# Two-layer cross-attention and mixture-of-experts kernel: where LN2's inverse deviation lies, who scales the identities, the order of copies and low parts, and the size of GpSimd's subtractions

## The chip, the cores and the metric

One core of a Trainium2 chip. The metric is the device time of one execution in microseconds (us). TensorE (PE), VectorE (DVE), ScalarE (ACT), GpSimd (POOL) and the queues of SyncE (SP) each follow their own list of instructions and meet through semaphores.

## The reference, cut to what matters

```
x: 4 x 256 x 256, context: 4 x 256 x 128
q, k   = ctx @ Wq.T + bq, ctx @ Wk.T + bk
x      = x + tanh(g_x) * (LN(x) contracted with softmax(q k^T))      # attention, 4 batches
y      = LN(x)                                                       # "LN2"
logits = gelu(y @ rw1) @ rw2;  probs = softmax;  top-2 of 8 experts
x      = x + tanh(g_f) * sum over the two choices of p_e * (gelu(y @ w1[e] + b1[e]) @ w2[e] + b2[e])
         (tokens that did not choose an expert get its constant term instead)
```

1024 tokens, hidden size 1024, 8 experts, exact GELU.

## The kernel before, in words

Attention and layer norms run over four batches b of 256 tokens (two tiles t of 128). Per batch: `energies` (PE), `maxima` (DVE), `exps` (ACT), `shares` (DVE: reciprocal of the row sums, then two scaled identities `diag`, 128x128, in SBUF), `probT_tr` (PE, a product with the scaled identity, which transposes and divides at once), `probT_copy` (ACT), `mix` (PE), `residual` (DVE), `second_stats` (DVE), `second_deviation` (ACT, a square root), `second_norm` (DVE: reciprocal of the deviation, then two subtract-and-multiply instructions into `lnx`), `xnT_tr` and `router_hidden` (PE), `router_gelu` (ACT), `router_logits` (PE). `first_pull` (DVE) makes the scale `pull` of LN1 and, by one more instruction, `shift`, which only the constant term at the end reads.

The expert weights come in 32 quarters of 128x1024 fp32 through `stage`, a ring of 6 slots filled by the SP queue in order. Each quarter is split in two: the high part `w_hi` (f16, a copy: `high` on ACT, `own` on POOL) and the low part `w_lo` (bf16, stage minus w_hi: `low` on DVE, line 685, whole quarters; `lows` on POOL, line 399, in pieces of `PIECE` columns). Quarter q+6 is fetched only when both parts of quarter q are done. `DVE_QUARTERS` says which low parts DVE makes, `POOL_HIGHS` which high parts POOL makes. `wait_weights(engine, q)` waits until the low parts up to q are done on both engines.

The normalised tokens are split in the same way (`token_high` on ACT, `token_low` on POOL, line 412) and sent to a table in DRAM (`send`, line 575, one per batch). After the router, DVE finds the two experts of each token and every token's slot by a chain of small instructions (lines 821 to 861), PE turns them into row numbers, and POOL gathers the tokens of each block of 128 from the table (line 427), which needs `index_ready` and all four `table_sent`.

Then blocks of 128 rows pass through their expert. Blocks 0 to 7 (one for each expert, written out) use the weights in SBUF, later blocks (a loop) have their first weight matrix fetched by number. In iteration i, PE does `tokens_tr(i+1)` (line 1254) and interleaves `up(i, c)` (lines 1280 to 1282) with `down(i-1, c)` (lines 1291 to 1293) over eight column groups c. Each half of a hidden block goes through `gelu_half` and `hidden_high` on ACT and `hidden_low` on DVE (line 938), and `down` waits for them at c = 0 and c = 4. DVE's iteration i is: `xT_copy(i+2)`, `hidden_low(i, second half)`, low parts, a piece of the index work (`rest_of_blocks`, `rest_of_indices`, `experts_of_blocks`, `used_counts`, lines 884 to 961), `hidden_low(i+1, first half)`, `y_copy(i)`. POOL's later order of gathers, low parts and scatters (`put`) is written out by hand.

Of the kernel before, what the change touches and what calls it, by code (L numbers as in the profile page):

```python
# [4 lines left out]
P = 128  # L5
# [3 lines left out]
T = TOK // P  # L9
# [20 lines left out]
PIECE = 256  # L30
# [15 lines left out]
def flamingo_moe_kernel(nc, x, ctx_in, g_x, g_f, Wq, bq, Wk, bk, rw1, rw2, w1, b1, w2, b2, consts, out):  # L46
# [6 lines left out]
    with ctx:  # L53
# [64 lines left out]
        shift = sb("shift", [P, T], F32)  # L118
# [110 lines left out]
        q_done, k_done, q_ready, k_ready = sem("q_done"), sem("k_done"), sem("q_ready"), sem("k_ready")  # L229
        energy, max_ready, exp_ready, prob_ready = sem("energy"), sem("max_ready"), sem("exp_ready"), sem("prob_ready")  # L230
# [22 lines left out]
        DVE_QUARTERS = (6, 7, 8, 13, 14, 15, 17, 19, 20, 23, 24, 26, 28, 29, 30, 31)  # L253
        POOL_HIGHS = (0, 1, 2, 3, 4, 5, 9)
# [135 lines left out]
        def _(pool):  # L390
# [60 lines left out]
            own(0, 6)  # L451
            token_low(0)
# [4 lines left out]
            lows(10, 13)  # L457
# [46 lines left out]
        def _(act):  # L504
# [36 lines left out]

            def probT_copy(b):
# [62 lines left out]
            second_deviation(1)  # L605
            high(7, 8)
            xnT_copy(0)
            token_high(0)
            second_deviation(2)
            high(8, 9)  # L610
            xnT_copy(1)
            second_deviation(3)
            router_gelu(0)
            router_gelu(1)
            token_high(1)
            xnT_copy(3)
# [6 lines left out]
            send(1)  # L623
            send(2)
            high(11, 12)
            send(3)
            high(12, 13)
# [3 lines left out]
            high(13, 18)  # L631
# [18 lines left out]
            for i in range(NS):  # L650
                for half in range(2):
                    gelu_half(i, i % 2, i, half)
                    hidden_high(i, i % 2, half)
                    q = 18 + 2 * i + half
                    high(q, min(q + 1, QUARTERS))
# [19 lines left out]
        def _(dve):  # L675
# [39 lines left out]
            def shares(b):  # L715
                dve.wait_ge(exp_ready, 2 * b + 2)
                step(nc.vector.reciprocal(rinv[:, 2 * b:2 * b + 2], rsum[:, 2 * b:2 * b + 2]))
                for j in range(2):
                    last = nc.vector.tensor_scalar(diag[:, b, j, :], ident, rinv[:, 2 * b + j:2 * b + j + 1],  # L719
                                                   None, ALU.mult)  # L720
                last.then_inc(prob_ready, 1)
# [15 lines left out]
            def first_pull(h):  # L737
                ts = slice(4 * h, 4 * h + 4)
                dve.wait_ge(std_ready, h + 1)
                if h == 0:  # L740
                    dve.wait_ge(tg_ready, 1)
                step(nc.vector.reciprocal(rstd[:, ts], rstd[:, ts]))
                step(nc.vector.tensor_scalar(pull[:, ts], rstd[:, ts], tg[:, 0:1], None, ALU.mult))
                nc.vector.scalar_tensor_tensor(out=shift[:, ts], in0=mv[:, ts, 0], scalar=-1.0, in1=pull[:, ts],
                                               op0=ALU.mult, op1=ALU.mult)
# [17 lines left out]
            def second_norm(b):  # L763
                dve.wait_ge(std_ready, b + 3)
                if b == 0:
                    dve.wait_ge(zero_sent, 32)
                step(nc.vector.reciprocal(rstd2[:, 2 * b:2 * b + 2], rstd2[:, 2 * b:2 * b + 2]))
                for t in (2 * b, 2 * b + 1):
                    nc.vector.tensor_scalar(lnx[:, t, :], xs[:, t, :], mv2[:, t, 0:1], rstd2[:, t:t + 1],  # L769
                                            ALU.subtract, ALU.mult).then_inc(xn_ready, 1)  # L770
# [37 lines left out]
            low(8)  # L808
# [73 lines left out]
            def rest_of_blocks():  # L882
                rank_te = rank_s[:, :].rearrange("p (t e) -> p t e", t=T)
# [5 lines left out]
                step(nc.vector.tensor_reduce(out=st_[:, :], in_=ltc, axis=X, op=ALU.add))  # L889
                step(nc.vector.tensor_tensor(out=slotb, in0=rank_te, in1=e_bc(st_[:, :]), op=ALU.add))  # L890
# [104 lines left out]
            low(13)  # L995
            low(14)
# [85 lines left out]
        def _(pe):  # L1082
# [216 lines left out]
            for i in range(NS):  # L1299
# [34 lines left out]
            wait_weights(pe, QUARTERS - 1)  # L1334
# [4 lines left out]
            jl, used = last_pair(pe), used_blocks(pe)  # L1339
            with pe.Fori(JS, JN - 1) as j:  # L1340
# [84 lines left out]
```

## Time and profile before

| what | value |
|---|---|
| median of 3 runs | 204.19 us (201.62 to 208.66) |
| the profiled execution: its own time | 201.4 us |
| its span, first to last instruction | 199.5 us |
| granted TensorE clock, mean | 0.939 |
| PE busy | 162.1 us (81%) |
| DVE busy | 137.9 us (69%) |
| POOL busy | 111.6 us (56%) |
| ACT busy | 101.7 us (51%) |

Busy times are sums over stages of different nature: attention and router up to 44 us, choice of experts up to 60 us, written-out blocks up to 112 us, the loop of blocks up to 179 us, and the sum of outputs. 1.9 us of the execution lie around the span.

### The profile page before, as it was taken

To read this page: it belongs to the slowest core of one execution; us is meant where nothing else is said; L and a number is where in the kernel's file an instruction comes from. 1 tells how busy PE (TensorE), PEld (TensorE's weight loads), DVE (VectorE), ACT (ScalarE), POOL (GpSimd) and SP (SyncE) were. 2 spreads that over 40 slices of the span, in tenths; PEclk is the share of its full clock that TensorE was granted. 3 is DMA by queue.
4 is the path that set the end of the run, shared out by engine and by line. 5 is a ranking of instruction groups with operands and counts; after the bars stand their busy time and mean duration, and the time that the engine had idled before them with its cause. 6 is when DMAs were issued, how large, how long until landed. Compare 5 with 4: busy or idle time off the path is not lost.

```text
span 199.5 us, 5205 instructions
## 1 busy us (share of the span) xinstructions
PE 162.1 (81%) x1722; PEld 137.3 (69%) x1723; DVE 137.9 (69%) x304; ACT 101.7 (51%) x249; POOL 111.6 (56%) x172
## 2 busy tenths in 40 slices
PE   6887984593838999789899499699499999998910
PEld 2456873371318999679899499599399999886600
DVE  2679999998843567997987256945656777364184
ACT  0695746777822999938978244233244334430000
POOL 0049999979975989565975605544255444113200
PEclk9999999999585899969999999999999999999975
DMA  6899453349997288737119426655267656431395
GB/s 186 242 385 353 124 199 106 105 114 369 369 276 269 78 263 258 229 104 252 57 49 375 154 80 225 251 210 228 71 237 253 230 221 217 193 145 33 102 332 219
DMA packets 21028, 40.69 MB, mean 204 GB/s; under 512 B 2741, under 2 KB 12047, under 8 KB 21010
## 3 DMA queue, kind: packets, MB, share of 16 engines
q1 hardware_dynamic: 17680, 34.54, 49.0%
q0 software_dynamic: 1872, 4.73, 7.6%
q10 hardware_dynamic: 1458, 1.19, 1.8%
q8 instruction: 10, 0.16, 0.3%
q14 instruction: 8, 0.07, 0.1%
HBM read 23.66 MB, written 4.60 MB: 142 GB/s over the span
## 4 chain that ended last, share of the span: by engine, by line
PE 47%; DVE 29%; DMA 9%; issue 7%; ACT 3%; DVEq 1%; SPq 1%; POOL 1%; POOLq 0%
PE bank L1280 7%; PE bank L1282 7%; PE bank L1281 7%; PE bank L1291 7%; PE bank L1292 6%; PE bank L1293 6%; DVE w_lo L685 3%; DVE lnx L769 3%; DMA probT<-x_table,gidx 3%; DMA cf<-in_ctx 2%; DVE qT L719 2%; DMA stage<-y_table 2%; DVE lnT L938 2%; DVE xs L750 2%; ACT bank L639 2%
## 5 line engine op out<-in xcount | busy, mean ns | idle before, releaser
L639 ACT ACTIVATE bank<-bank,b1T 128x128 f32<-128x128 f32 x152 | 42.4, 342 | 56.8 <-PE bank L1282 56.6
L1291 PE MATMUL bank<-w_hi,cf 128*128 (+1 forms) x152 | 41.7, 275 | 7.9 <-DVE lnT L938 7.2
L399 POOL TENSOR_TENSOR w_lo<-stage,w_hi 128x256 bf16<-128x256 f32 x64 | 44.0, 720 | 0.9 <-ACT w_hi L515 0.2
L1292 PE MATMUL bank<-w_lo,cf 128*128 (+1 forms) x152 | 41.7, 275 | 0.0
L1293 PE MATMUL bank<-w_hi,lnT 128*128 (+1 forms) x152 | 41.7, 274 | 0.0
L1280 PE MATMUL bank<-cfT,stage 128*128 128x128 f16 x176 | 34.0, 219 | 0.0
L1282 PE MATMUL bank<-cfT,stage 128*128 128x128 f16 x176 | 34.0, 219 | 0.0
L1281 PE MATMUL bank<-cfT,stage 128*128 128x128 bf16 x176 | 34.0, 219 | 0.0
L938 DVE TENSOR_TENSOR lnT<-bank,cf 128x512 bf16<-128x512 f32 x38 | 26.2, 690 | 6.7 <-ACT cf L646 4.0
L416 POOL TENSOR_TENSOR held<-cst 128x1 f32<-128x1 f32 x31 | 6.0, 193 | 41.8 <-DVE lnx L951 40.7
L515 ACT ACTIVATE w_hi<-stage 128x1024 f16<-128x1024 f32 x25 | 26.2, 1049 | 3.2 <-DMA stage<-in_L_ffn_w 1.9
L1280 PE MATMUL bank<-cfT,w_hi 128*128 128x128 f16 x128 | 27.2, 233 | 0.6 <-DVE cfT L929 0.6
L1281 PE MATMUL bank<-cfT,w_hi 128*128 128x128 bf16 x128 | 27.3, 234 | 0.0
L1282 PE MATMUL bank<-cfT,w_lo 128*128 128x128 f16 x128 | 27.2, 234 | 0.0
L945 DVE CAST cf<-bank 128x512 f16<-128x512 f32 x22 | 15.1, 688 | 16.0 <-issue 9.8
L685 DVE TENSOR_TENSOR w_lo<-stage,w_hi 128x1024 bf16<-128x1024 f32 x16 | 21.4, 1369 | 0.0
L1291 PEld LDWEIGHTS bank<-w_hi,cf 128*128 128x128 f16 x152 | 15.0, 99 | 8.2 <-issue 7.4
L1280 PEld LDWEIGHTS bank<-cfT,stage 128*128 128x128 f16 x176 | 17.2, 98 | 0.9
L1281 PEld LDWEIGHTS bank<-cfT,stage 128*128 128x128 f16 x176 | 17.2, 98 | 0.9
L1282 PEld LDWEIGHTS bank<-cfT,stage 128*128 128x128 bf16 x176 | 17.2, 98 | 0.0
L929 DVE COPY cfT<-bank 128x256 int32<-128x256 int32 x20 | 8.4, 419 | 12.6 <-PE bank L1256 9.4
L1293 PEld LDWEIGHTS bank<-w_hi,lnT 128*128 128x128 bf16 x152 | 15.0, 98 | 1.8
(196 smaller groups left out, 341.9 us busy)
## 6 DMA issues: line engine op xcount, KB each, us to landing
stage<-in_L_ffn_w SPq DMA_DIRECT2D x32, 512.0 KB, 5.5
stage<-w_hi SPq DMA_DIRECT2D x12, 512.0 KB
stage<-w_lo SPq DMA_DIRECT2D x12, 512.0 KB
stage<-y_table SPq DMA_DIRECT2D x8, 256.0 KB, 4.3
xs<-in_x SPq DMA_DIRECT2D x2, 512.0 KB, 7.3
out<-stage SPq DMA_DIRECT2D x4, 256.0 KB, 2.8
cf<-in_ctx SPq DMA_DIRECT2D x1, 512.0 KB, 4.9
x_table<-cfT ACTq DMA_DIRECT2D x2, 256.0 KB, 5.6
```

The costliest lines, as they stand in the source:

```text
L399: last = nc.gpsimd.tensor_tensor(out=w_lo[:, q, n:n + PIECE], in0=stage[:, q % RING, n:n + PIECE], in1=w_hi[:, q, n:n + PIECE], op=ALU.sub ...
L515: nc.scalar.activation(w_hi[:, q, :], stage[:, q % RING, :], ACT.Copy).then_inc(hi_ready, 1)
L639: last = nc.scalar.activation(h, h, ACT.Gelu, bias=bias)
L685: nc.vector.tensor_tensor(out=w_lo[:, q, :], in0=stage[:, q % RING, :], in1=w_hi[:, q, :], op=ALU.subtract).then_inc(lo_dve, 1)
L938: nc.vector.tensor_tensor(out=h_lo[:, u, cs, :], in0=hidden_of(u, half), in1=h_hi[:, u, cs, :], op=ALU.subtract).then_inc(h_ready, 1)
L945: nc.vector.tensor_copy(h_hi[:, u, 4 * half:4 * half + 4, :], hidden_of(u, half)).then_inc(hh_ready, 1)
L1280: mm(o, wh, xh[:, d, :], start=(d == 0), stop=False)
L1281: mm(o, wh, xl[:, d, :], start=False, stop=False)
L1282: last = mm(o, wl, xh[:, d, :], start=False, stop=(d == DC - 1))
L1291: mm(o, h_hi[:, u, c, :], w2_hi[:, ex, 1, c, :], start=(c == 0), stop=False)
L1292: mm(o, h_hi[:, u, c, :], w2_lo[:, ex, 1, c, :], start=False, stop=False)
L1293: last = mm(o, h_lo[:, u, c, :], w2_hi[:, ex, 1, c, :], start=False, stop=(c == HC - 1))
```

## The change

`PIECE` goes from 256 to 512. LN2's reciprocal is written to PSUM (the start of the bank that the batch's `mix` used), and the normalisation becomes a scalar_tensor_tensor whose second tensor is that PSUM column, broadcast. The scaled identities move to ACT, after a new semaphore `rinv_ready` from DVE's reciprocal. `shift` is no longer made in `first_pull`; the instruction that writes the last column of `cat` makes it at the end. On ACT the copies of attention and LN2 (`xnT_copy`) go ahead of `high` and `token_high`, and one `high` more stands between `send`s. The low parts are dealt anew and, on DVE, one of them stands ahead of each `hidden_low` of the second half; the index work of iteration 2 is divided over iterations 1 and 2, and `used_counts` moves from iteration 5 to 4. PE waits for the weights of `down` in two steps, runs `rest_of_codes` at c = 1, not 3, and loads its registers for the loop before it waits for the last weights.

```
-PIECE = 256
+PIECE = 512
-DVE_QUARTERS = (6, 7, 8, 13, 14, 15, 17, 19, 20, 23, 24, 26, 28, 29, 30, 31)
-POOL_HIGHS = (0, 1, 2, 3, 4, 5, 9)
+DVE_QUARTERS = (6, 7, 11, 12, 13, 15, 17, 19, 20, 22, 23, 26, 28, 29, 30, 31)
+POOL_HIGHS = (0, 1, 2, 3, 4, 5, 9, 27)

 POOL:
 own(0, 6)
+lows(8, 9)
 token_low(0)
 own(9, 10)
 token_low(1); token_low(2); token_low(3)
-lows(10, 13)
+lows(10, 11)
...
+lows(14, 15)
+refill(6, 0, 2, 16)
 lows(16, 17)
-refill(6, 0, 2, 16)
-lows(18, 19)
 wait(yidx_ready, 1); put(0, 0); refill(7, 1, 3, 16)
+lows(18, 19)
+put(1, 1)
 lows(21, 22)
-put(1, 1)
-lows(22, 23)
 put(2, 0)
-lows(25, 26)
-put(3, 1)
-lows(27, 28)
+lows(24, 25)
 wait(index_ready, 2)
 refill(NS, 0, 4, 32)
+put(3, 1)
+lows(25, 26)
+own(27, 28)
 put(4, 0)

 ACT:
+def shares(b):
+    act.wait_ge(rinv_ready, b + 1)
+    for j in range(2):
+        last = nc.scalar.activation(diag[:, b, j, :], ident, ACT.Copy, scale=rinv[:, 2 * b + j:2 * b + j + 1])
+    last.then_inc(prob_ready, 1)
 exps(0); project(1)
+shares(0)
 exps(1)
+shares(1)
 probT_copy(0); exps(2)
+shares(2)
 exps(3); probT_copy(1)
+shares(3)
 ...
-high(7, 8)
 xnT_copy(0)
-token_high(0)
+high(7, 8)
 second_deviation(2)
-high(8, 9)
 xnT_copy(1)
+high(8, 9)
 second_deviation(3)
 router_gelu(0); router_gelu(1)
-token_high(1)
+token_high(0)
 xnT_copy(3)
+token_high(1)
 ...
 send(1)
+high(11, 12)
 send(2)
-high(11, 12)
+high(12, 13)
 send(3)
-high(12, 13)

 DVE:
 def shares(b):
     dve.wait_ge(exp_ready, 2 * b + 2)
-    step(nc.vector.reciprocal(rinv..., rsum...))
-    for j in range(2):
-        last = nc.vector.tensor_scalar(diag[:, b, j, :], ident, rinv[:, 2 * b + j:2 * b + j + 1], None, ALU.mult)
-    last.then_inc(prob_ready, 1)
+    nc.vector.reciprocal(rinv..., rsum...).then_inc(rinv_ready, 1)
 def second_norm(b):
-    step(nc.vector.reciprocal(rstd2[:, 2 * b:2 * b + 2], rstd2[:, 2 * b:2 * b + 2]))
+    inverse = bank[3 + b][:, 0:2]
+    step(nc.vector.reciprocal(inverse, rstd2[:, 2 * b:2 * b + 2]))
     for t in (2 * b, 2 * b + 1):
-        nc.vector.tensor_scalar(lnx[:, t, :], xs[:, t, :], mv2[:, t, 0:1], rstd2[:, t:t + 1], subtract, mult)
+        nc.vector.scalar_tensor_tensor(out=lnx[:, t, :], in0=xs[:, t, :], scalar=mv2[:, t, 0:1],
+            in1=inverse[:, t % 2:t % 2 + 1].broadcast_to([P, D]), op0=subtract, op1=mult)
-low(8)                                  # ahead of the choice of experts: low(6), low(7) stay
-low(13); low(14)                        # after the row numbers
+low(11); low(12)
 ...
-low(15)
+low(13)
-between = {0: (17,), 1: (19, 20), 2: (), 3: (23, 24), 4: (26,), 5: (28, 29), 6: (30, 31)}
+ahead = {0: (15,), 1: (19,), 2: (20,), 3: (22,), 4: (23,), 5: (26,), 6: (30,)}
+behind = {0: (17,), 5: (28, 29), 6: (31,)}
 for i in range(NS - 1):
     xT_copy(i + 2, u)
+    for q in ahead[i]: low(q)
     hidden_low(i, u, 1)
-    for q in between[i]: low(q)
+    for q in behind.get(i, ()): low(q)
+    i == 1: rest_of_starts()     # the first four instructions of what was rest_of_blocks
     i == 2: rest_of_blocks()     i == 3: rest_of_indices()
-    i == 4: experts_of_blocks()  i == 5: used_counts()
+    i == 4: experts_of_blocks(), used_counts()

 PE:
-if c == 0: wait_weights(pe, QPE * i - 1)
+if c % 4 == 0: wait_weights(pe, QPE * i - 2 + c // 4)
-if i == 4 and c == 3: ... rest_of_codes()
+if i == 4 and c == 1: ... rest_of_codes()
-wait_weights(pe, QUARTERS - 1)
 pe.wait_ge(eb_ready, 1)
 (two register loads, wait for used_ready, two more)
+wait_weights(pe, QUARTERS - 1)
```

## Rows read from the trace of the kernel before

**Rows 1.** Windows over blocks 0, 2, 4 and 7: busy by engine, granted clock, DMA.

```profile
60.69:65.90 5.21, 5.21 (x50) 5.21 (x51) 2.08 (x3) 2.42 (x6) 3.58 (x4) 0.50 0.55 200
...
71.67:77.19 5.52, 5.52 (x79) 5.25 (x76) 4.41 (x6) 5.16 (x13) 4.54 (x7) 1.00 0.79 241
...
82.71:92.31 9.60, 7.55 (x95) 6.83 (x93) 8.86 (x20) 5.32 (x13) 4.86 (x6) 0.82 0.51 160
...
104.25:112.33 8.08, 5.53 (x78) 5.00 (x74) 4.74 (x7) 6.08 (x16) 4.89 (x7) 1.00 0.82 309
```

**Rows 2.** The chain that ended last, around the gather: start, us, what.

```profile
53.34 0.17 DVE gidx L861
...
53.79 5.64 DMA probT<-x_table,gidx
```

**Rows 3.** DVE's timeline, 20 to 45 us: start, us, line, operation.

```profile
21.12 0.58 DVE L743 TENSOR_SCALAR pull<-rstd,tg 128x4 f32<-128x4 f32 x1
21.73 0.59 DVE L744 SCALAR_TENSOR_TENSOR shift<-mv,pull 128x4 f32<-128x4 f32 x1
...
23.58 0.86 DVE L750 SCALAR_TENSOR_TENSOR xs<-bank,pull,xs 128x256 f32<-128x256 f32 x2
...
26.70 1.69 DVE L769 TENSOR_SCALAR lnx<-xs,mv,rstd 128x256 f32<-128x256 f32 x2
...
37.74 1.24 DVE L769 TENSOR_SCALAR lnx<-xs,mv,rstd 128x256 f32<-128x256 f32 x2
...
39.50 5.44 DVE L685 TENSOR_TENSOR w_lo<-stage,w_hi 128x1024 bf16<-128x1024 f32 x3
```

**Rows 4.** DVE's instructions grouped by line and form: busy us, mean ns.

```profile
L769 DVE TENSOR_SCALAR lnx<-xs,mv,rstd 128x256 f32<-128x256 f32 x8 | 6.4, 835 | 0.1
L719 DVE TENSOR_SCALAR qT<-cst,rinv 128x128 f32<-128x128 f32 x8 | 5.3, 699 | 0.1
...
L750 DVE SCALAR_TENSOR_TENSOR xs<-bank,pull,xs 128x256 f32<-128x256 f32 x8 | 3.4, 469 | 0.0
```

**Rows 5.** ACT's timeline: the third load of a function table, and the last send.

```profile
20.93 1.28 ACT L580 ACT_TABLE_LOAD   x1
...
45.98 0.33 ACTq L575 DMA_DIRECT2D x_table<-probT  x1
```

**Rows 6.** The page's group of ACT's 128x128 activations.

```profile
L639 ACT ACTIVATE bank<-bank,b1T 128x128 f32<-128x128 f32 x152 | 42.4, 342 | 56.8 <-PE bank L1282 56.6
```

**Rows 7.** The DMA view, sends of the table: count, KB each, us to landing.

```profile
x_table<-probT ACTq DMA_DIRECT2D x2, 256.0 KB, 5.4
```

**Rows 8.** POOL's timeline, 32 to 46 us.

```profile
32.07 2.56 POOL L399 TENSOR_TENSOR w_lo<-stage,w_hi 128x256 bf16<-128x256 f32 x4
34.59 1.16 POOL L412 TENSOR_TENSOR cfT<-lnx,cfT 128x512 bf16<-128x512 f32 x1
...
42.02 3.93 POOL L412 TENSOR_TENSOR probT<-lnx,probT 128x512 bf16<-128x512 f32 x2 [1.40 <-ACT probT L571]
```

**Rows 9.** PE's timeline: the router's last product, and two waits (in brackets) between blocks.

```profile
43.01 0.61 PE L1176 MATMUL bank<-rw_s,qT 128*128 128x8 f32 x4
...
85.48 0.27 PE L1291 MATMUL bank<-w_hi,cf 128*128 128x256 f16 x1 [2.04 <-DVE lnT L938]
...
112.33 0.28 PE L1254 MATMUL bank<-ident,probT 128*128 128x128 f16 x2 [2.55 <-issue]
```

**Rows 10.** DVE's timeline in the written-out blocks.

```profile
73.32 0.69 DVE L938 TENSOR_TENSOR lnT<-bank,cf 128x512 bf16<-128x512 f32 x1 [0.69 <-ACT cf L646]
...
80.39 1.69 DVE L887 TENSOR_TENSOR lnx<-cst,more 128x72 f32<-128x72 f32 x1
...
84.65 0.68 DVE L938 TENSOR_TENSOR lnT<-bank,cf 128x512 bf16<-128x512 f32 x1
...
107.84 1.22 DVE L685 TENSOR_TENSOR w_lo<-stage,w_hi 128x1024 bf16<-128x1024 f32 x1
```

**Rows 11.** SP's timeline: the first fetch of a looped block's weights.

```profile
103.63 0.52 SPq L356 DMA_DIRECT2D stage<-w_hi  x1
```

More of the change, by code:

```diff
@@ L540, in exps @@
                                          accum_out=rsum[:, 2 * b + j:2 * b + j + 1]).then_inc(exp_ready, 1)
+            def shares(b):
+                act.wait_ge(rinv_ready, b + 1)
+                for j in range(2):
+                    last = nc.scalar.activation(diag[:, b, j, :], ident, ACT.Copy,
+                                                scale=rinv[:, 2 * b + j:2 * b + j + 1])
+                last.then_inc(prob_ready, 1)
             def probT_copy(b):
@@ L605, in _ @@
             second_deviation(1)
+            xnT_copy(0)
             high(7, 8)
-            xnT_copy(0)
-            token_high(0)
             second_deviation(2)
+            xnT_copy(1)
             high(8, 9)
-            xnT_copy(1)
             second_deviation(3)
@@ L630, in _ @@
             nc.scalar.activation(warm[:, 2:3], tg[:, 0:1], ACT.Gelu)
-            high(13, 18)
+            high(13, 17)
             def gelu_half(i, u, e, half):
@@ L653, in _ @@
                     hidden_high(i, i % 2, half)
-                    q = 18 + 2 * i + half
+                    q = 17 + 2 * i + half
+                    if q >= 27:
+                        q += 1
                     high(q, min(q + 1, QUARTERS))
@@ L716, in shares @@
                 dve.wait_ge(exp_ready, 2 * b + 2)
-                step(nc.vector.reciprocal(rinv[:, 2 * b:2 * b + 2], rsum[:, 2 * b:2 * b + 2]))
-                for j in range(2):
-                    last = nc.vector.tensor_scalar(diag[:, b, j, :], ident, rinv[:, 2 * b + j:2 * b + j + 1],
-                                                   None, ALU.mult)
-                last.then_inc(prob_ready, 1)
+                nc.vector.reciprocal(rinv[:, 2 * b:2 * b + 2], rsum[:, 2 * b:2 * b + 2]).then_inc(rinv_ready, 1)
             def lnT_copy(b):
@@ L743, in first_pull @@
                 step(nc.vector.tensor_scalar(pull[:, ts], rstd[:, ts], tg[:, 0:1], None, ALU.mult))
-                nc.vector.scalar_tensor_tensor(out=shift[:, ts], in0=mv[:, ts, 0], scalar=-1.0, in1=pull[:, ts],
-                                               op0=ALU.mult, op1=ALU.mult)
             def residual(b):
@@ L990, in constant_sum @@
                 nc.vector.tensor_tensor(out=cat[:, :, 0:N_EXP], in0=dcat[:, 0, :, :], in1=dcat[:, 1, :, :], op=ALU.add)
-                nc.vector.tensor_copy(cat[:, :, 2 * N_EXP:CAT], shift[:, :].unsqueeze(2))
+                nc.vector.scalar_tensor_tensor(out=cat[:, :, 2 * N_EXP:CAT], in0=mv[:, :, 0:1], scalar=-1.0,
+                                               in1=pull[:, :].unsqueeze(2), op0=ALU.mult, op1=ALU.mult)
                 nc.vector.tensor_tensor(out=cat[:, :, N_EXP:2 * N_EXP], in0=wprod[:, 0, :, :], in1=wprod[:, 1, :, :],
                                         op=ALU.add).then_inc(cat_ready, 1)
-            low(13)
-            low(14)
+            low(11)
+            low(12)
             scatter_rows(0, N_EXP)
@@ L1008, in _ @@
                 xT_copy(i + 2, u)
+                for q in ahead[i]:
+                    low(q)
                 hidden_low(i, u, 1)
-                for q in between[i]:
+                for q in behind.get(i, ()):
                     low(q)
-                if i == 2:
+                if i == 1:
+                    rest_of_starts()
+                elif i == 2:
                     rest_of_blocks()
@@ L1306, in _ @@
                     if i:
-                        if c == 0:
-                            wait_weights(pe, QPE * i - 1)
+                        if c % 4 == 0:
+                            wait_weights(pe, QPE * i - 2 + c // 4)
                         down(i - 1, 1 - u, i - 1, c)
-                        if i == 4 and c == 3:
+                        if i == 4 and c == 1:
                             pe.wait_ge(y_ready, 3)
```

14 lines of the change are left out of this document (7 added, 7 removed).

## The prediction

> **What bounds the kernel now.** I read the table of busy times first: PE is busy for 81%, so the blocks should be PE's and everything else a chain. The windows over single blocks bear this out [rows 1]: block 2 takes 5.52 us with PE busy throughout at full clock, block 4 takes 9.60 and block 7 takes 8.08, with PE idle for 2.0 and 2.5 us of them. PE's own timeline names the two waits [rows 9]: 2.04 us for DVE's low part of a hidden half, 2.55 us of "issue", which is PE's sequencer on register loads. Block 0 runs at half clock [rows 1]. Ahead of the blocks I followed the chain of waits: DVE from the residuals to the choice of experts, then the row numbers at 53.34 + 0.17 = 53.51, the gather from 53.79 [rows 2], and the first product of block 0 at 60.69. DVE is the bound there, and part of its time is no work: normalising 128x256 takes 0.84 us on average, while a two-tensor instruction of the same size, one of its tensors in PSUM, takes 0.47; a 128x128 scaling takes 0.70; even 4 columns of `pull` and of `shift` take 0.58 and 0.59 [rows 3, 4]. So instructions wholly in SBUF wait here for something, and POOL is subtracting all the while in pieces of 0.64 (2.56 for four) [rows 8]. In the blocks it is the same: 72 columns took 1.69 us [rows 10].
>
> **Attention and LN2.** DVE loses the eight scalings (5.3 us of busy time by the group; back to back a little less), two `shift`s (0.55 each on the path) and about 0.4 us of each of eight normalisations, 3.1 us in all if they cost what the residual's instruction costs [rows 4]. Not all of it shortens the path. ACT takes eight scalings. No row has ACT at 128x128 from SBUF; its nearest, 128x128 in PSUM, is 0.34 [rows 6], pipelined 0.28 to 0.3, so I take 0.3 to 0.35 each, 2.6 us in all, and the ends 0.25 and 0.5. Three of the four pairs also make a round trip (ACT's exps, DVE's reciprocal, ACT again), some 0.4 us in which ACT waits, and behind it are queued the next exps, the copies of `probT` and the square root with its table load, which was at 20.93 [rows 5]. Placing these by hand, the load comes at 22.5 to 22.8, 1.7 us later. On DVE the first residual was at 23.58 [rows 3]; now it follows the last reciprocal, at about 21.6. From there to the last normalisation's end at 37.74 + 1.24 = 38.98 [rows 3] it was 15.4 us; take off 0.55 for a `shift`, 3.1 for the normalisations, and add 2.2 for three places where DVE now runs out of work and waits for ACT's square roots. It ends at 21.6 + 13.95 = 35.6, 3.4 us earlier.
>
> From that end to the router's last product it took 4.64 us (43.01 + 0.61 [rows 9]), all of it PE and ACT, which now have their copies first: 40.2. DVE has its two low parts done by then, at the 1.81 us each of the three that stood there (5.44 / 3 [rows 3]): from 36.2 to 39.8. The choice of experts began at 39.50 + 5.44 = 44.94 and needs 53.51 - 44.94 = 8.57 us, all the same after: the row numbers are there at about 48.9, 4.6 us earlier.
>
> **The table takes over.** The gather needs the four sends too, and they hang on POOL. The last `token_low` ended at 42.02 + 3.93 = 45.95, the last send went at 45.98 [rows 5, 8] and landed 5.4 us later [rows 7], at 51.4, two us before it was needed. POOL's new list up to that `token_low` has one quarter more (`lows(8, 9)`), which waits for ACT's high part at about 33.7. Two pieces of 512 should cost what the `token_low` of 512 columns costs, 1.16 each [rows 8]: 2.3 for 2.56, so 0.26 off each of seven quarters, 1.8 in all, and 2.3 more for quarter 8. DVE's low parts fall into the same stretch: the `token_low`s that met them took 1.97, not 1.16 [rows 8]. I get the last `token_low` at 44.5 (no collision) to 46.5 (both low parts in the way) and take 45.5; ACT's sends stand behind three `high`s of about 1.05, ready at 44.9, and so don't decide. Sent at 45.8, landed at 51.2 to 51.5, gather at 51.8 for 53.79: **2.0 us gained** (1.0 to 3.3), not 4.6. PE then idles longer ahead of block 0; it is at half clock there anyway.
>
> **The blocks.** In iteration 2, DVE's index work kept the low part of block 3's first half until 84.65 [rows 10]. Four of its instructions, some 2.8 us, move to iteration 1, whose second low part goes; the low part then comes near 82.3, ahead of PE's need at 83.4. Block 4 gives back the wait of 2.04 and the half clock that followed it: 9.60 less 5.52 and less 0.6 for `rest_of_codes`, so **3.5 us** (2 to 3.6) [rows 1, 9].
>
> Against it: the low part moved ahead of each `hidden_low`. DVE sat idle there for 0.69 us until ACT was done [rows 10]; the low part takes 1.22 alone [rows 10] and 1.81 beside POOL. `hidden_low` comes 0.4 to 1.1 us late, and behind it wait the low part of the next half, `y_copy` and PE's `down` at c = 4. By the same timelines PE's slack there is 0.5 to 0.8. So nothing is lost where POOL is silent and up to 0.5 where it subtracts; iteration 1 with its four small instructions is the tightest, and low(29), behind three low parts, has 0.6 us left before block 7. I put **0.8 us** on this, from 0 to 3.
>
> Block 7's 2.55 us: the last low part ended at 107.84 + 1.22 = 109.06 [rows 10] and only then did PE's sequencer begin its loads, which lasted to 112.33 [rows 9], 3.3 us. With the wait behind them they start as soon as the queue has taken block 7's last products. How far ahead the sequencer is no row shows: at least the 0.7 us of work it had left at 109.06. The ends are a gain of 0 and of 2.55; two such loads in the loop of blocks cause no gap on PE, so I take 1.0. A full gain would soon meet the fetch for block 8, issued at 103.63 [rows 11], now one low part later.
>
> Later steps cost about nothing: POOL's 16 quarters are 4 us shorter under other waits, `shift` in `cat` has 8 columns, and the loop of blocks and the end are unchanged, PE-bound at 5.5 us a block.
>
> **Sum.** 201.4 - 2.0 - 3.5 + 0.8 - 1.0 = 195.7 for an execution like the profiled one. That one lies at the low end of the three runs, 2.8 us below their median. Some of this excess will be in the other median too; I take half: **197.0 us**, against 204.19.
>
> **A rule that speaks against the change.** The rows above show waiting instructions and a POOL that works in pieces. The Trainium skill, "SBUF — State Buffer", section "Who interferes with whom", says that the loser of the pair of ports that VectorE and GpSimd share waits for the winner's whole instruction. The trace agrees with waits of up to one or two pieces (1.69 us for 72 columns). By this rule a piece of 512 makes each remaining wait up to 0.5 us longer.
>
> **The rivals.**
> (A) Longer pieces hurt the blocks. DVE's low parts ahead of `hidden_low`, and the index work, wait for pieces of 1.16 instead of 0.64. For: DVE took 1.81 a quarter beside POOL's 512-column instructions. Against: in the blocks most low parts took 1.22, and POOL has pauses. If each of five iterations stalls PE by 1.2 us over its slack and the clock falls after each as in block 4 (1.5 us each, from 9.60 - 6.1 - 2.04), it costs 13.5 us: 201.4 - 2.0 - 3.5 - 1.0 + 13.5 = 208.4, slower; it decides from about 2 us a stall, when the clock goes too. Chance 0.07. Without loss of the clock (5 x 0.9 = 4.5 us) it is 199.4, with the excess 200.8, no change: 0.18.
> (B) The normalisation in its new form waits as before, the change doesn't do what it says. LN2 keeps its 3.1 us, the row numbers come at 52.0, the gather at 52.3 and not 51.8: 196.2, with the excess 197.5. The table hides nearly all of this. Chance 0.1.
> (C) The table isn't the bound, as POOL's shorter quarters bring it forward: gather at 49.2, 193.1, or 194.4 with the excess. Chance 0.15.
> (D) The gain at the front is spent: ACT becomes the bound in attention (scalings at 0.5, round trips at 0.6), the gather stays at 53.5, and iteration 1 stalls: 201.4 - 0.3 - 2.0 + 0.8 = 199.9, about 201 with the excess. Chance 0.1.
> My forecast: 0.4.
>
> **Range and chances.** Forecast, B and C lie between 192 and 200; A without the clock and D at 200 to 202. The range 192 to 202.5 leaves out A with the clock and the best ends. Two per cent, about what a measurement can tell from no change here, is 4.1 us, so 200.1 is the border. Faster: 0.4 + 0.1 + 0.15, and a little of A and D: 0.68; same 0.25; slower 0.07.
>
> **What would show it.** Normalisations of 0.45 to 0.5 us each; ACT's scalings at 0.3 to 0.35; a first residual near 21.6; row numbers near 49 and a gather that starts 2 to 3 us after them, released by the last send; no wait of 2 us on PE in block 4 and full clock in it; the gap before block 8 under 2 us. I would be wrong if DVE's low parts in the blocks take 1.8 us or more and PE waits for `hidden_low` in blocks 2 to 7, if POOL's 512-column pieces cost more than 1.3 us, or if the sends land before the row numbers.

## The result and the profile after

The changed kernel is slower by 1.3%: 204.86 us, median of 20 runs, against 202.88 for the kernel before on the same chip (20 runs); ratio 1.013, 95% interval 1.009 to 1.017. Here and below the medians take all executions and the ratios only those that did not fall into a slower state, so a ratio is not the quotient of the medians beside it. Forecast was 197.0 with a range of 192 to 202.5. The profiled executions stand at 204.87 (span 202.8) and 201.4 (span 199.5), so the traces have 3.3 us of span to explain.

**The front gained more than was forecast, in part by another way.** DVE's timeline, the group of the normalisations and ACT's group of the scaled identities (busy us, mean ns), and the sends of the table (KB each, us to landing):

```profile
21.99 0.86 DVE L759 SCALAR_TENSOR_TENSOR xs<-bank,pull,xs 128x256 f32<-128x256 f32 x2
...
34.50 0.87 DVE L779 SCALAR_TENSOR_TENSOR lnx<-xs,mv,bank 128x256 f32<-128x256 f32 x2
...
42.89 0.22 DVE L831 TENSOR_REDUCE top<-bank 128x8 f32<-128x64 f32 x1 [3.39 <-PE bank L1193]
...
51.38 0.16 DVE L871 SCALAR_TENSOR_TENSOR gidx<-code,bank 128x8 int32<-128x8 f32 x1
...
L779 DVE SCALAR_TENSOR_TENSOR lnx<-xs,mv,bank 128x256 f32<-128x256 f32 x8 | 3.5, 478 | 0.1
...
L547 ACT ACTIVATE qT<-cst,rinv 128x128 f32<-128x128 f32 x8 | 2.8, 394 | 0.9 <-DVE rinv L732 0.9
...
x_table<-probT ACTq DMA_DIRECT2D x2, 256.0 KB, 3.6
```

The normalisations cost 478 ns where they cost 835 [rows 4]; the last ends at 35.37, where it was 38.98 [rows 3]. The row numbers, though, come at 51.54, only 2.0 us earlier. DVE waited 3.39 us for the router. The reason is in PE's timeline and the windows:

```profile
32.57 1.13 PE L1186 MATMUL bank<-kT,rw_s 128*128 128x256 f32 x4 [1.45 <-ACT kT L567]
34.43 2.10 PE L1174 MATMUL bank<-cst,lnx 128*128 128x128 f32 x8 [0.73 <-DVE lnx L779]
...
37.04 2.05 PE L1186 MATMUL bank<-kT,rw_s 128*128 128x256 f32 x4
...
35.00:41.00 6.00, 6.00 (x22) 5.12 (x21) 4.29 (x4) 3.22 (x8) 5.43 (x4) 0.50 0.34 103
```

After the gaps of 1.45 and 0.73, TensorE's granted clock is 0.50 (1.2 of 2.4 GHz) from 35 to 41, and four router products take 2.05 us instead of 1.13. The last send goes at 46.11, where it went at 45.98 [rows 5], and by the view's 3.6 us (5.4 before [rows 7]) it lands at about 49.7, before the row numbers; the gather starts at 51.83 and block 0's tokens reach PE at 54.79, 4.7 us before the 59.47 of the kernel before. From the gather's start to its first rows it took 3.0 us, not 5.7.

**The blocks lost it again.** Windows, one row for each of blocks 0 to 7 (columns as in [rows 1]):

```profile
55.87:60.83 4.96, 3.06 (x53) 2.91 (x53) 2.00 (x3) 2.66 (x6) 3.37 (x4) 1.00 0.90 294
60.83:67.33 6.50, 5.68 (x79) 5.27 (x77) 6.08 (x4) 5.33 (x13) 6.30 (x6) 1.00 0.56 176
67.33:74.22 6.89, 5.69 (x79) 5.26 (x77) 5.68 (x11) 5.28 (x13) 3.82 (x5) 1.00 0.75 235
74.22:79.74 5.52, 5.52 (x78) 5.25 (x76) 5.32 (x5) 5.27 (x13) 5.34 (x6) 1.00 0.57 158
79.74:88.24 8.50, 6.08 (x94) 5.66 (x92) 8.16 (x18) 5.27 (x13) 4.29 (x5) 1.00 0.71 241
88.24:94.15 5.91, 5.69 (x78) 5.26 (x76) 5.84 (x9) 5.28 (x13) 5.22 (x7) 1.00 0.40 124
94.15:105.55 11.40, 7.36 (x78) 6.56 (x76) 9.83 (x19) 5.31 (x13) 8.26 (x9) 0.85 0.35 112
105.55:113.22 7.67, 5.70 (x79) 5.17 (x76) 4.74 (x7) 5.96 (x16) 4.28 (x7) 1.00 0.86 319
```

The same blocks took 5.53, 5.52, 5.52, 9.60, 5.52, 6.26 and 8.24 (blocks 1 to 7) before. Block 4 gives back 1.1 us, block 6 costs 5.1, blocks 1 and 2 cost 1.0 and 1.4. The lead of 5.3 us at block 1 is a lag of 0.9 at block 8. PE's timeline names what it waited for, and its group view sums it up:

```profile
82.88 0.27 PE L1308 MATMUL bank<-w_hi,cf 128*128 128x256 f16 x1 [2.42 <-DVE lnT L950]
...
98.95 0.27 PE L1308 MATMUL bank<-w_hi,cf 128*128 128x256 f16 x1 [4.04 <-DVE lnT L950]
...
113.22 0.28 PE L1271 MATMUL bank<-ident,probT 128*128 128x128 f16 x2 [1.98 <-issue]
...
PE bank L1308 <- DVE lnT L950: 13.4, 7, 4.0
```

Seven waits for `hidden_low`, 13.4 us in all; before there were four, 7.2 us. In blocks 1 and 2 PE waited 0.82 us (at 65.02) and 1.20 (at 69.25), behind two low parts of DVE that now stand near POOL's gathers and subtractions; alone a low part takes 1.22 [rows 10]:

```profile
61.60 2.68 DVE L700 TENSOR_TENSOR w_lo<-stage,w_hi 128x1024 bf16<-128x1024 f32 x1
...
64.80 3.71 DVE L700 TENSOR_TENSOR w_lo<-stage,w_hi 128x1024 bf16<-128x1024 f32 x1
...
65.12 2.29 POOL L399 TENSOR_TENSOR w_lo<-stage,w_hi 128x512 bf16<-128x512 f32 x2
```

What held DVE in the later blocks is seen when its timeline is laid beside POOL's, which is the main reading of this case:

```profile
77.00 3.09 DVE L902 TENSOR_TENSOR lnx<-rank_s,st_ 128x64 f32<-128x64 f32 x1
80.13 0.23 DVE L903 SCALAR_TENSOR_TENSOR lnx<-rank_s,lnx 128x64 f32<-128x64 f32 x1
...
85.45 2.31 DVE L882 TENSOR_SCALAR yt<-code 128x16 f32<-128x16 f32 x1
87.68 0.16 DVE L883 TENSOR_SCALAR yt<-code 128x16 f32<-128x16 f32 x1
...
91.55 3.81 DVE L921 TENSOR_TENSOR en<-en,cst 128x8 f32<-128x8 f32 x1
```

```profile
76.69 1.01 POOL L446 DMA_INDIRECT y_table<-lnx,yidx  x1 [0.16 <-issue]
77.72 2.29 POOL L399 TENSOR_TENSOR w_lo<-stage,w_hi 128x512 bf16<-128x512 f32 x2
...
85.41 2.31 POOL L399 TENSOR_TENSOR w_lo<-stage,w_hi 128x512 bf16<-128x512 f32 x2
...
91.04 1.00 POOL L446 DMA_INDIRECT y_table<-lnx,yidx  x1 [0.16 <-issue]
92.06 2.28 POOL L399 TENSOR_TENSOR w_lo<-stage,w_hi 128x512 bf16<-128x512 f32 x2
94.28 1.05 POOL L406 CAST w_hi<-stage 128x1024 f16<-128x1024 f32 x1
```

Eight columns of `en` take 3.81 us, and end at 95.36; POOL's unbroken run (issue of the scatter, two pieces, the cast) ends at 95.33. The other two: 80.09 against 80.01, 87.76 against 87.72. Once DVE is through, its next instruction of the same kind takes 0.16 to 0.23. So in these three cases DVE did not get in at the border between two pieces; it waited until POOL's run was over.

### The profile page after: what moved, and what is told of

Its sections match the earlier page's. It is cut to its first block, busy times and chain, and to the rows that moved or that the text cites. A ratio compares the mean times of both kernels' runs of the same rounds, so it can differ in the third digit from the quotient of the medians.

```text
span 202.8 us, 5180 instructions
## 1 busy us (share of the span) xinstructions
PE 165.6 (82%) x1722; PEld 139.8 (69%) x1723; DVE 137.4 (68%) x294; ACT 102.3 (50%) x256; POOL 107.7 (53%) x141
## 3 DMA queue, kind: packets, MB, share of 16 engines
q10 hardware_dynamic: 1458, 1.19, 1.7%
## 4 chain that ended last, share of the span: by engine, by line
PE 49%; DVE 28%; issue 7%; DMA 7%; ACT 4%; POOL 1%; DVEq 1%; SPq 1%; POOLq 0%
PE bank L1308 6%; PE bank L1298 6%; PE bank L1299 6%; PE bank L1297 6%; PE bank L1310 6%; PE bank L1309 6%; DVE w_lo L700 4%; PE bank L1105 3%; DMA probT<-x_table,gidx 3%; DVE lnT L950 3%; DMA stage<-y_table 3%; DVE en L921 2%; PE bank L1186 2%; DVE lnx L902 1%; DVE lnx L779 1%
## 5 line engine op out<-in xcount | busy, mean ns | idle before, releaser
L1308 PE MATMUL bank<-w_hi,cf 128*128 (+1 forms) x152 | 42.3, 278 | 13.4 <-DVE lnT L950 13.4
L399 POOL TENSOR_TENSOR w_lo<-stage,w_hi 128x512 bf16<-128x512 f32 x32 | 36.6, 1169 | 2.2 <-ACT w_hi L517 1.5
L1297 PE MATMUL bank<-cfT,stage 128*128 128x128 f16 x176 | 34.7, 222 | 0.0
L1298 PE MATMUL bank<-cfT,stage 128*128 128x128 bf16 x176 | 34.7, 222 | 0.0
L1299 PE MATMUL bank<-cfT,stage 128*128 128x128 f16 x176 | 34.6, 222 | 0.0
L416 POOL TENSOR_TENSOR held<-cst 128x1 f32<-128x1 f32 x31 | 8.3, 269 | 47.4 <-DVE lnx L963 46.4
L1297 PE MATMUL bank<-cfT,w_hi 128*128 128x128 f16 x128 | 25.1, 223 | 0.6 <-DVE cfT L941 0.6
L517 ACT ACTIVATE w_hi<-stage 128x1024 f16<-128x1024 f32 x24 | 24.9, 1047 | 0.9 <-POOL cfT L412 0.9
L1299 PE MATMUL bank<-cfT,w_lo 128*128 128x128 f16 x128 | 25.2, 224 | 0.0
L1298 PE MATMUL bank<-cfT,w_hi 128*128 128x128 bf16 x128 | 25.2, 224 | 0.0
L700 DVE TENSOR_TENSOR w_lo<-stage,w_hi 128x1024 bf16<-128x1024 f32 x16 | 24.3, 1534 | 0.0
L1309 PEld LDWEIGHTS bank<-w_lo,cf 128*128 128x128 f16 x152 | 15.1, 99 | 1.5 <-issue 1.4
```

The lines of the kernel that those rows point to most:

```text
L399: last = nc.gpsimd.tensor_tensor(out=w_lo[:, q, n:n + PIECE], in0=stage[:, q % RING, n:n + PIECE], in1=w_hi[:, q, n:n + PIECE], op=ALU.sub ...
L517: nc.scalar.activation(w_hi[:, q, :], stage[:, q % RING, :], ACT.Copy).then_inc(hi_ready, 1)
L700: nc.vector.tensor_tensor(out=w_lo[:, q, :], in0=stage[:, q % RING, :], in1=w_hi[:, q, :], op=ALU.subtract).then_inc(lo_dve, 1)
L1297: mm(o, wh, xh[:, d, :], start=(d == 0), stop=False)
L1298: mm(o, wh, xl[:, d, :], start=False, stop=False)
L1299: last = mm(o, wl, xh[:, d, :], start=False, stop=(d == DC - 1))
```

## The experiments

**My theory**: a DVE instruction wholly in SBUF waits to the end of POOL's unbroken run, and the index work pays for that; its cure is operands in PSUM. (Experiments 1 and 3 refute "to the end" as a rule, experiment 5 bears out the rest.) **Rivals**: the length of a piece alone is the price (a wait to the next border); the low part ahead of each `hidden_low` makes it late; the half clock in the router. Each kernel was compared with the kernel before on the same chip; the chips differ between groups of experiments, so two experiments are compared here by the difference of their ratios.

**1. The changed kernel with pieces of 256**

```
-PIECE = 512
+PIECE = 256
```

> The changed kernel with GpSimd's pieces back at 256 columns. Theory P (a VectorE instruction wholly in SBUF waits for GpSimd's running stream, and two long pieces leave it one chance to get in where four leave three): the waits of the changed kernel's blocks (2.68 and 3.71 us for two low parts, 3.09 for the 64 columns of line 902, 3.81 for 8 columns of line 921) fall to 2 us or less each, PE's 13.4 us of waits for hidden low parts to 9 or less, and the time by 2.5 to 4.5 us, to about 199 to 201. Theory O (the new order of low parts and index work is the cause, whatever the size): time within 1 us of the changed kernel, waits as long.

201.7 us (before 202.76), ratio 0.995 (0.991 to 1.000). Against the change's 1.013 the pieces of 512 cost 1.8%, 3.6 us. But the wait stays (DVE, then POOL; the profiled execution took 204.78, 3 us above this median):

```profile
94.28 3.51 DVE L921 TENSOR_TENSOR en<-en,cst 128x8 f32<-128x8 f32 x1
```

```profile
94.22 2.56 POOL L399 TENSOR_TENSOR w_lo<-stage,w_hi 128x256 bf16<-128x256 f32 x4
96.71 1.05 POOL L406 CAST w_hi<-stage 128x1024 f16<-128x1024 f32 x1
```

Three borders between pieces went by unused, and the one before the cast too. A low part of 2.88 us stayed as well, and PE's waits for `hidden_low` were 11.1 us where at most 9 were expected. Shorter pieces help the first low parts (1.32 and 1.31 us for 2.68 and 3.71) and line 902 (0.78), hardly line 921. A wait to the next border (0.64) is refuted as the rule; so is a wait to the end of the run, for line 903 (79.40 to 81.33) and line 882 (86.79 to 88.75) got in ahead of the last of four pieces, which ended at 81.86 and 89.32.

**2. The kernel before with pieces of 512**

```
-PIECE = 256
+PIECE = 512
```

> The kernel before with pieces of 512 columns and nothing else. Theory P: LN2 and the scaled identities are still in SBUF, so the chain to the row numbers gets longer (eight normalisations and eight scalings wait for pieces of 1.14 us instead of 0.66), and so do the waits in blocks: 3 to 6 us slower than before. Theory O: the size matters little, within 1.5 us of before.

Its runs scatter from 201.05 to 207.28 (median 206.18), so no ratio is given and neither expectation is decided. Its profile, of the fastest of them, has the same mark in the old order, one 64-column instruction of the index work:

```profile
77.39 2.90 DVE L884 TENSOR_TENSOR lnx<-nexp,cst 128x64 f32<-128x64 f32 x1
```

**3. The low parts back behind `hidden_low`**

```
-ahead = {0: (15,), 1: (19,), 2: (20,), 3: (22,), 4: (23,), 5: (26,), 6: (30,)}
-behind = {0: (17,), 5: (28, 29), 6: (31,)}
+ahead = {}
+behind = {0: (15, 17), 1: (19,), 2: (20,), 3: (22,), 4: (23,), 5: (26, 28, 29), 6: (30, 31)}
```

> The changed kernel with every low part of VectorE's block iterations put behind the hidden low part instead of one ahead of it; pieces stay at 512. Theory O: the low part ahead is what makes PE wait; PE's waits at c = 4 go (0.8, 1.2 us and less), the time falls by 1.5 to 3 us. Theory P: the long waits for GpSimd only move to another place, the time falls by less than 1 us, and the wait of 3.8 us in experts_of_blocks stays.

203.64 us, ratio 1.004 (1.000 to 1.009), 0.9% or some 1.7 us better than the change; the two intervals all but touch. That is the size that the rival had foretold (1.5 to 3), not mine (below 1). But PE still waits 11.7 us for `hidden_low`, in six pieces: the order is worth something, and the rest of the waits fall on other instructions. Blocks 1 and 2 come back to 5.53 and 6.09 us, and block 6 rises to 13.15. In the same profile lines 902 and 903 wait for one piece each, and get in at the border in the middle of POOL's run and at its end:

```profile
69.75 3.02 DVE L896 TENSOR_TENSOR lnx<-cst,more 128x72 f32<-128x72 f32 x1
...
76.08 1.17 DVE L902 TENSOR_TENSOR lnx<-rank_s,st_ 128x64 f32<-128x64 f32 x1
77.29 1.08 DVE L903 SCALAR_TENSOR_TENSOR lnx<-rank_s,lnx 128x64 f32<-128x64 f32 x1
```

```profile
75.94 2.35 POOL L399 TENSOR_TENSOR w_lo<-stage,w_hi 128x512 bf16<-128x512 f32 x2
```

So a wait may end at the next border or miss it. In the 14 traces an index or normalising instruction of DVE missed a border 19 times (15 to 115 us), and each time it began within the issue of an indirect DMA on POOL or at most 0.4 us behind it; those that began later got in at the next border. Some that began as near got in too, and low parts missed borders farther from an issue. What decides is not shown.

**4. Filler products between the router's**

```
 xnT_tr(1)
+keep_busy(6, 7, filler)
 router_hidden(1)
+keep_busy(4, 7, filler)
 xnT_tr(2)
```

> The changed kernel with ten filler products (128x512, into an unused bank) on PE in the two gaps ahead of the router's second and third batch. Theory C (PE's clock was halved from 34 to 41 us because PE had little work between 31 and 34): the granted clock stays at 1.0 there, the choice of experts begins 2 to 2.5 us earlier than at 42.9, but the gather then hangs on the last send, so that the row numbers come near 49.3 and the gather starts only some 0.3 us earlier: time within 1 us of the changed kernel. Rival: the table is no bound and the gather starts 2 us earlier too.

The clock holds and the row numbers come at 48.94 instead of 51.54. First the window, then the gather, then a product at the end of the kernel:

```profile
33.00:41.00 8.00, 7.67 (x48) 5.86 (x48) 6.97 (x16) 7.20 (x13) 6.80 (x6) 1.00 0.50 160
```

```profile
50.90 1.70 POOL L427 DMA_INDIRECT probT<-x_table,gidx  x1 [2.65 <-DMA x_table<-probT]
...
184.14 1.18 PE L1365 MATMUL bank<-xs,cst 128*128 128x512 f32 x2 [2.04 <-issue]
```

The gather gains 0.9 us of 2.6, as the table takes over, and block 0's tokens come 1.1 us later (55.91), since the gathered rows land 5.0 us after the issue. The whole is slower, 208.55, ratio 1.028 (1.021 to 1.035), where I had expected it within 1 us of the change. Some 3 us are lost at the very end, in code that the edit doesn't touch: PE's "issue" wait of 2.04 us is followed by half clock (0.50 from 186 to 188.3), where the change has one of 0.83 and keeps full clock. Why that wait is longer is open.

**5. The index work of iterations 1 to 4 through PSUM**, in columns of banks 2 and 3 that are idle there; pieces stay at 512

```
+more_p = bank[3][:, D:D + N_EXP + 1];  st_p = bank[2][:, D:D + N_EXP]
+code_p, yt_p = bank[3][:, D:D + REST], bank[3][:, D + REST:D + 2 * REST]
-step(nc.vector.tensor_tensor(out=slotb, in0=rank_te, in1=e_bc(st_[:, :]), op=ALU.add))
+step(nc.vector.tensor_tensor(out=slotb, in0=rank_te, in1=e_bc(st_p), op=ALU.add))
... (slotb, rslot, blk_i, en, ebf, used_f, code and yt of these steps in the same way)
```

> The changed kernel with VectorE's index work of iterations 1 to 4 rewritten so that nearly every instruction has one operand or its output in an idle PSUM bank (three more small reductions, some 0.7 us); pieces stay at 512, the order of everything stays. Theory P (the waits are for GpSimd's stream, and only instructions wholly in SBUF have them): 3.09 us of line 902, 2.31 of line 882 and 3.81 of line 921 fall below 0.5 each, PE's wait of 4.0 us in block 6 goes, and the time falls by 3 to 5 us, to 200 to 202. Rival (those instructions wait for something else, such as DMA traffic or the sequencer): the same waits with their operands in PSUM, time as of the changed kernel.

199.4 us against 204.26, ratio 0.993 (0.983 to 1.004), so not to be told from the kernel before; 2.0% below the change's ratio, whose interval lies apart. The instruction that waited 3.81 us meets POOL in the same place, and doesn't notice:

```profile
88.96 0.17 DVE L933 TENSOR_TENSOR bank<-bank,cst 128x8 f32<-128x8 f32 x1
89.17 0.35 DVE L935 TENSOR_TENSOR lnx<-cst,bank 128x192 f32<-128x192 f32 x1
...
94.08 3.69 DVE L700 TENSOR_TENSOR w_lo<-stage,w_hi 128x1024 bf16<-128x1024 f32 x2
```

```profile
88.18 1.00 POOL L446 DMA_INDIRECT y_table<-lnx,yidx  x1 [0.16 <-issue]
89.20 2.29 POOL L399 TENSOR_TENSOR w_lo<-stage,w_hi 128x512 bf16<-128x512 f32 x2
...
92.54 4.14 POOL L399 TENSOR_TENSOR w_lo<-stage,w_hi 128x512 bf16<-128x512 f32 x2
```

Block 6 is back at 5.52 us and PE's waits for `hidden_low` fall from 13.4 to 7.3. One index instruction, of 256 columns, kept both inputs in SBUF, and it alone still waits, 1.19 us beside a piece, for 0.42 in experiment 1:

```profile
78.58 1.19 DVE L922 TENSOR_TENSOR lnx<-lnx,cst 128x256 f16<-128x256 f16 x1
```

This is the theory's own test, and in this it holds: for these instructions the place of the operands decides whether there is a wait. Blocks 1 and 2 stay at 6.50 and 6.87 us: they have no index work with a long wait, but the low parts. These are what is left and can't leave SBUF: 3.69 for two beside POOL, whose own two pieces then take 4.14, not 2.29.

**6. The change with LN2's normalisation back in SBUF**

```
-inverse = bank[3 + b][:, 0:2]
-step(nc.vector.reciprocal(inverse, rstd2[:, 2 * b:2 * b + 2]))
+step(nc.vector.reciprocal(rstd2[:, 2 * b:2 * b + 2], rstd2[:, 2 * b:2 * b + 2]))
-nc.vector.scalar_tensor_tensor(..., in1=inverse[...].broadcast_to([P, D]), op0=subtract, op1=mult)
+nc.vector.tensor_scalar(lnx[:, t, :], xs[:, t, :], mv2[:, t, 0:1], rstd2[:, t:t + 1], subtract, mult)
```

> The changed kernel with LN2's normalisation as it was, in SBUF, beside pieces of 512. Prices the PSUM form alone. Theory P: each normalisation takes 0.8 to 1.3 us instead of 0.44, the last one ends 3 to 5 us later than at 35.3, and the row numbers come 2 to 4 us later, less what PE's half clock in the router had cost. Rival (it does nothing, the chain is bound elsewhere): row numbers within 0.5 us of the changed kernel's 51.5.

210.31 us, ratio 1.050 (1.035 to 1.064); the group of the normalisations:

```profile
L778 DVE TENSOR_SCALAR lnx<-xs,mv,rstd 128x256 f32<-128x256 f32 x8 | 8.4, 1085 | 0.1
```

Beside pieces of 512 the SBUF form costs 1085 ns (835 beside pieces of 256 [rows 4]), against 478. The row numbers come at 56.59, 5.1 us later than the change's (2 to 4 expected), block 0's tokens at 59.82. The PSUM form is worth 3.7% of the time here, and without it the longer pieces would have hurt the front too.

**7. The kernel before with the front's DVE and ACT edits alone** (scaled identities on ACT, reciprocal in PSUM, no `shift`; lists of copies and low parts as before)

```
-step(nc.vector.reciprocal(rinv..., rsum...))            # DVE, and two tensor_scalar into diag
+nc.vector.reciprocal(rinv..., rsum...).then_inc(rinv_ready, 1)
+shares(b) on ACT; inverse and scalar_tensor_tensor as in the change
```

> The kernel before with only the attention and LN2 part of the change: scaled identities on ScalarE, inverse deviation in PSUM, no shift; all orders, the dealing of low parts and the pieces of 256 stay. Theory P: row numbers 1.5 to 2.5 us earlier than 53.5 (PE's half clock and a third low part ahead of the choice take part of 3.4), no new waits in the blocks, time 1 to 2.5 us below before. Rival: GpSimd's table or PE's clock takes all of it, time within 0.5 us of before.

202.81 us, ratio 1.010 (0.998 to 1.021): nothing gained, where 1 to 2.5 us were expected, although the row numbers come at 49.0, 4.5 us earlier than before. POOL issues the gather, and three quarters stood ahead of it in its list:

```profile
54.38 1.12 POOL L427 DMA_INDIRECT probT<-x_table,gidx  x1 [0.17 <-issue]
```

So the front needs the new list of POOL (`lows(10, 11)`, not `lows(10, 13)`) as much as the faster DVE.

**8. Experiment 5 with pieces of 256 from the first gather on**, 512 ahead of it, where DVE works in PSUM

```
+def lows(a, b, piece=PIECE):   # and 256 given for quarters 14, 16, 18, 21, 24, 25 and those after 20 of own
```

> The changed kernel with the index work through PSUM and pieces of 256 columns from the gathers on, 512 ahead of them. If theory P holds for both: the gain of pieces of 256 (3 us) and of the index work (3 to 5) overlap, 4.5 to 6.5 us below the changed kernel, 198.5 to 200.5, faster than the kernel before by 1 to 2%. If pieces of 256 only helped the index work, as the index work through PSUM alone.

196.69 us, ratio 0.977 (0.962 to 0.993), a little more than the 1 to 2% expected.

**9. The same again**, with more runs, on another chip.

> The changed kernel with the index work through PSUM and pieces of 256 columns from the gathers on, a second time in five rounds, for its interval. Theory P: 2 to 3.5% below the kernel before. Rival (its first measurement was luck of the clock): within 1% of before.

197.46 us against 203.86, ratio 0.981 (0.972 to 0.990). This is the fastest version found: 2% below the kernel before, 3% below the change.

**10. The change again**, on that chip.

> The changed kernel itself, on the same chip. 0.5 to 1.5% above before. Its profile shows whether the half clock near 145 us, which cost it some 1.6 us against the profile of before, comes every time (a cause in the change) or not (chance).

205.3 us, against 203.86, ratio 1.016 (1.000 to 1.031). Its profile repeats the waits within 0.01 us (3.10, 2.32, 3.81 for lines 902, 882, 921): they are the schedule's, not chance. The half clock near 145 us is there again too (0.51 from 144 to 147).

**11. Version 8 with the low parts behind `hidden_low`**, the edit of experiment 3.

> The version with the index work through PSUM and pieces of 256 in the blocks, but with every low part of VectorE behind the hidden low part. Theory O (the low part ahead delays PE): 1 to 2 us faster than with it ahead, PE's waits for hidden low parts shorter. Theory P (with short waits the order hardly matters): within 1 us.

197.96 us, ratio 0.986 (0.981 to 0.992): not to be told from 9. With the index work out of SBUF and pieces of 256 the order makes no difference that could be measured.

**12. Version 8 with pieces of 128 in the blocks**

```
-lows(14, 15, 256)   # and the others
+lows(14, 15, 128)
```

> As the version with the index work through PSUM, with pieces of 128 columns from the gathers on. GpSimd needs some 0.5 us more for a quarter (0.66 for 256 and 1.14 for 512 give about 0.18 us for the start of each piece). If VectorE gets in at nearly any border of pieces, its low parts wait less: 1.2 to 1.5 us each for 1.2 to 2.5, and the time stays within 1 us of that with 256. If VectorE misses borders, however many there are, its low parts still take over 2 us beside GpSimd.

202.79 us, ratio 1.011 (1.003 to 1.020). POOL's group and PE's longest wait:

```profile
L399 POOL TENSOR_TENSOR w_lo<-stage,w_hi 128x128 bf16<-128x128 f32 x56 | 29.1, 557 | 0.2
```

```profile
94.95 0.29 PE L1316 MATMUL bank<-cfT,w_hi 128*128 128x128 f16 x1 [4.42 <-POOL w_lo L399]
```

POOL is busy for 29.1 us with its seven quarters, 4.2 us each, where version 8 with four pieces each took 22.9, or 3.3, and PE now waits for POOL: 0.9 us more for a quarter, not the 0.5 expected. DVE gains nothing by it, its low parts take 1.58 us on average for 1.51. 256 is better than 128 here. Against 512 (experiment 5, ratio 0.993 for 0.981 in 9) it looks better too, but these two intervals overlap.

## Why the prediction was wrong

The step that failed is "I put **0.8 us** on this, from 0 to 3", the price of the low part ahead of `hidden_low` beside POOL; longer pieces got a price only in rival A. It measured 7.9 us, as DVE's waits for POOL ran over several of POOL's instructions. Its terms against the profiles:

| term | forecast | measured |
|---|---|---|
| start of block 0's tokens, and block 0 | -2.0 | -4.7 and -0.6 |
| block 4 | -3.5 | -1.1 |
| the other blocks, 1 to 6 | +0.8 | +7.9 |
| block 7, register loads | -1.0 | -0.6 |
| after block 8 | 0 | +2.4 |
| sum | -5.7 | +3.3 |

**The blocks.** I priced a wait at one piece, 1.16 instead of 0.64, and took slack of 0.5 to 0.8 us to absorb it. Blocks 1 and 2 lost 2.3 us behind low parts of 2.68 and 3.71 us, blocks 5 and 6 5.5. The Trainium skill's rule ("SBUF — State Buffer", "Who interferes with whom": the loser waits for the winner's whole instruction) was cited for "up to 0.5 us longer"; the traces agree with it where a wait ended at the next border (1.17 us in experiment 3), and go beyond it with index instructions of 2.3 to 3.8 us over several of POOL's (1.9 to 3.5 with pieces of 256). Another rule of the Trainium skill in that section is that a VectorE instruction with at most one SBUF input, "outside the 2-port perf modes", does not contend with GpSimd. It is borne out by 0.17 and 0.35 us for lines 933 and 935 of experiment 5, during POOL's issue and its next piece. Line 882 has its one input in SBUF too, and waited (2.31 us); in which mode it ran no trace shows. Rival A came nearest, and I gave it 0.25 in all; its stalls were priced by one piece, and its two sums take different ones (1.2 us and 0.9). What I held against it ("in the blocks most low parts took 1.22, and POOL has pauses") looked at the low parts, not at the index work, and row 80.39 of [rows 10], 72 columns in 1.69 us, already showed an index instruction waiting over more than one piece of 0.64.

**Block 4.** Here a second step failed, the full gain of 3.5 us. The four instructions did move, but the rest of `rest_of_blocks` begins with line 902, which met POOL's run and took 3.09 us. PE's wait in block 4 went from 2.04 to 2.42. The gain of 1.1 is the clock, which held at 1.00 this time (0.82 before [rows 1]).

**Block 6.** `used_counts` moved into the iteration of `experts_of_blocks`, and `own(27, 28)`'s cast was added to POOL's run right there. The wait of 3.81, with two more in `experts_of_blocks` and `used_counts` (0.63 and 0.89 for lines 926 and 971), brought PE's of 4.04, and the half clock that followed it the rest. Experiment 5 shows that the wait is what cost block 6; the move and the cast weren't taken back one by one.

**The front.** ACT's scalings took 0.39 (0.3 to 0.35 forecast), the first residual came at 21.99 (21.6), the last normalisation ended at 35.37 (35.6): right but for sizes. The row numbers were 2.6 us late (51.5, not 48.9), by the half clock in the router, which I had not looked for and which experiment 4 removes. The gather came at 51.83 where I had 51.8, but that was luck: I had it released by the last send, landed at 51.2 to 51.5, and it was released by the row numbers, the send having landed at about 49.7. In experiments 4, 5 and 9 the row numbers come earlier and the gathers do wait for the table, but start at 49.1 to 50.9. The gain was larger than the gather's 2.0 us since the first rows landed 3.0 us after its issue, not 5.7, and block 0 ran at full clock. That is luck as well. It goes with the load of the DMA engines, which were busy for 0.32 of that time, and for 0.84 in the kernel before, while experiments 4 and 9 with 0.80 and 0.83 needed 5.0 and 5.5 us again. That the load is the cause is likely, but was not tested.

**Register loads.** 2.55 to 1.98 us, 0.6 for 1.0: mechanism right, size off.

**Signs.** Two of my three signs of being wrong came: low parts of more than 1.8 us with PE waiting for `hidden_low`, and sends that landed before the row numbers. The third did not, POOL's pieces of 512 took 1.17 us on average.

**After block 8** I had nothing. 1.65 us is a stretch of half clock at 144 to 147, after a wait of PE for DVE that both kernels have (2.83 after). Whether it belongs to the change is open. Both profiles of the change have it, and so have experiments 3 and 7, the latter of the family of the kernel before; versions 8 and 9 are one program, and only the profile of 9 has it, so it isn't fixed by the program alone. 0.7 us at the end wasn't traced.

**What each part is worth**, by the runs: the PSUM form of LN2 3.7% (6 against the change), pieces of 512 throughout -1.8% (1), the index work in SBUF beside them -2.0% (5), low parts ahead -0.9% (3), nothing measurable once the index work is in PSUM and the pieces are 256 (11). These are measured one at a time and don't add up.

## What to carry to other kernels

Where VectorE and GpSimd both work in SBUF, a wait of VectorE may be as short as to the next border between two of GpSimd's instructions and as long as GpSimd's unbroken run (its DMA issues and casts included); take the run as the upper bound, above all behind the issue of an indirect DMA. The small instructions of a chain lose most for their length, and one operand in idle PSUM frees them. Choose the size of GpSimd's pieces by stage: here 512 columns cost time in the blocks, and 128 made GpSimd the bound. Whether 512 gains anything at the front, where VectorE works in PSUM, was not measured by itself. When a step is moved, lay the two engines' timelines over each other at the new place; the average of the old one says little.

## What the runs showed of the hardware beyond that

- DVE waited through the issue of an indirect DMA on POOL as well: line 921 began at 91.55 within the issue of 91.04 + 1.00, and would have been over at 91.72 by the 0.17 of its twin in experiment 5. In the kernel before, line 884 (79.50 to 80.11) took 0.61 us for the 0.21 of its twin, line 893, in the change, all but its end within an issue (79.00 to 80.02). Not every part of an issue holds DVE: line 919, with both inputs in SBUF, took 0.16 us at 91.36, in the same issue as line 921.
- Reductions with input and output in SBUF didn't wait: line 925 took 0.35 us at 95.78, during POOL's piece from 95.41 on, and line 926 behind it, a TENSOR_SCALAR, 0.63.
- The contention goes both ways: two of POOL's pieces took 4.14 us instead of 2.29 beside two low parts of DVE.
- A piece on POOL takes 390 ns for 128 columns (3.12 for eight undisturbed in experiment 12; 557 on average, with contention), 640 for 256 (2.56 for four) and 1140 for 512 (2.29 for two): about 0.14 us of each is start, by the line through them.
- The granted clock fell after PE's wait of 4.04 us in block 6 (0.85 in that window), but held at 1.00 after one of 2.42 in block 4; behind a wait of 2.8 near 138 it fell in the profile of 9 (0.50 from 138 to 141) and held in that of 8 (1.00).
